# dt's projection in strips of 32 steps beside the gated recurrence, and four of the convolution's sixteen taps on POOL

## The reference

```python
def step(h, xs):                                   # gated recurrence, 128 steps
    z = sigmoid(xzt + h @ U_z + vz)
    r = sigmoid(xrt + h @ U_r + vr)
    hh = tanh(xht + r * h @ U + vh)
    return (1 - z) * h + z * hh
# Mamba block on x = the recurrence's states G
zxbcdt = x @ W_in                                  # 256 z, 384 xBC, 8 dt
dt = softplus(zxbcdt[..., -8:] + dt_bias)
xBC = depthwise_causal_conv(xBC, kernel, taps=16) + conv_b
xBC = silu(xBC)                                    # xs 256, B 64, C 64
dA = exp(dt * A)
h = h * dA + dt * x * B;  y = h @ C + D * xs       # a scan over the steps
y = y * silu(z);  y = rms_norm(y) * norm_w;  t = y @ W_out
x = x + (t / sqrt(1 + t * t)) @ W_nl + b_nl + G
```

## Time and profile before

| | us |
|---|---|
| median of three runs | 2279.24 (2276.68 to 2282.23) |
| profiled execution, its own time | 2276.11 |
| its span from first to last instruction | 2274.4 |
| recurrence | about 30 to 249 |
| Mamba block | about 249 to 700 |
| the rest | about 700 to 2274 |

### The profile page before, as it was taken

The page is one execution under the profiler, slowest core; times in us unless marked ns, Lnnn a source line. Parts: engine busy times, 40 slices in busy tenths (PEclk is TensorE's granted clock), DMA queues, the critical chain, the costliest instruction groups (busy, mean ns, idle before and its releaser), DMA issues.

```text
span 2274.4 us, 74250 instructions
## 1 busy us (share of the span) xinstructions
PE 2000.1 (88%) x31569; PEld 1323.4 (58%) x31675; DVE 1705.3 (75%) x3808; ACT 1001.4 (44%) x2827; POOL 458.8 (20%) x793
## 2 busy tenths in 40 slices
PE   7888888998886888787799999985999789999998
PEld 5555534444454555553567677763666456677776
DVE  3444489999965878787888888843999668888887
ACT  2333236566652121221455555542554445555555
POOL 2211000000000434335012122243432112121200
PEclk9999699999978899898899999996999999999999
DMA  2000000000010000000311111106553211111111
GB/s 61 4 3 4 1 1 1 1 1 1 1 38 17 2 3 2 3 3 2 111 48 44 44 44 44 39 4 128 107 108 73 65 40 44 39 44 44 44 57 37
DMA packets 76083, 77.35 MB, mean 34 GB/s; under 512 B 15756, under 2 KB 57060, under 8 KB 74180
## 3 DMA queue, kind: packets, MB, share of 16 engines
q1 hardware_dynamic: 71848, 70.11, 12.1%
q10 hardware_dynamic: 3904, 2.49, 0.4%
HBM read 60.09 MB, written 11.82 MB: 32 GB/s over the span
## 4 chain that ended last, share of the span: by engine, by line
PE 24%; DVE 18%; ACT 6%; issue 5%; DMA 1%; ACTq 1%; SPq 1%; POOL 1%; another core or an unknown queue 0%; POOLq 0%; DVEq 0%
PE B L85 23%; DVE work L2097 4%; DVE hr L2061 3%; DVE work L2105 3%; DVE work L107 2%; ACT hr L103 2%; ACT ltc L103 2%; ACTq L2384 1%; ACT catt L103 1%; DVE lth L107 1%; DVE lh L107 1%; DVE lpq L107 1%; ACT work L103 1%; DVE gr L1911 1%; DVE work L1471 1%
## 5 line engine op out<-in xcount | busy, mean ns | idle before, releaser
L85 PE MATMUL B<-gr,wres 128*128 128x512 f32 x1248 | 353.3, 411 | 16.4 <-DVE work L2105 10.2
L103 ACT ACTIVATE work<-B 128x512 f32<-128x512 f32 (+5 forms) x460 | 233.3, 524 | 124.4 <-PE B L85 69.3
L2147 POOL COPY G<-lh 128x32 f32<-128x32 f32 x256 | 148.2, 579 | 680.3 <-DVE lh L107 680.3
L85 PE MATMUL B<-work 128*128 128x128 bf16 (+3 forms) x1408 | 259.6, 312 | 28.3 <-ACT work L103 7.0
L85 PEld LDWEIGHTS B<-gr,wres 128*128 128x128 f32 x1248 | 214.2, 189 | 83.4 <-DVE work L2105 27.8
L103 ACT ACTIVATE hr<-work 128x512 fp32r<-128x512 f32 x272 | 172.9, 636 | 146.6 <-DVE work L2105 76.7
L85 PEld LDWEIGHTS B<-work 128*128 128x128 bf16 (+2 forms) x1408 | 141.3, 127 | 138.8 <-issue 79.5
L2061 DVE TENSOR_TENSOR hr<-work,hr 128x512 fp32r<-128x512 f32 x272 | 186.5, 686 | 8.1 <-ACT hr L103 6.6
L2097 DVE TENSOR_TENSOR work<-work 128x512 f32<-128x512 f32 x256 | 178.7, 698 | 14.0 <-ACT work L103 6.6
L107 DVE SCALAR_TENSOR_TENSOR work<-work,cw 128x512 f32<-128x512 f32 x240 | 179.2, 746 | 5.9
L85 PE MATMUL B<-hr,wres 128*128 128x512 f32 x624 | 177.9, 394 | 1.0 <-DVE hr L2061 1.0
(11 more groups left out here) (254 smaller groups left out, 3790.2 us busy)
## 6 DMA issues: line engine op xcount, KB each, us to landing
work<-wdr SPq DMA_DIRECT2D x128, 256.0 KB, 3.1
scr<-catt SPq DMA_DIRECT2D x144, 64.0 KB
work<-scr SPq DMA_DIRECT2D x16, 384.0 KB
work<-scr SPq DMA_DIRECT2D x16, 192.0 KB
catt<-in_L_ffn_ew SPq DMA_DIRECT2D x24, 128.0 KB, 2.4
work<-scr SPq DMA_DIRECT2D x16, 128.0 KB
out<-work SPq DMA_DIRECT2D x32, 64.0 KB, 2.2
work<-in_x ACTq DMA_DIRECT2D x2, 512.0 KB, 5.3
```

Of the source, the lines that this page charges most:

```text
L85: return e.matmul(out, lhsT, rhs, start=start, stop=stop, skip_group_check=True)
L103: return e.activation(out, in_, func, bias=bias, scale=scale)
L2147: e.tensor_copy(self.G[:, :, t], self.lh[:, t % 4, :]).then_inc(*inc("l.pool", "h", li, t))
```

## The change

- The convolution's taps are split 5 + 4 + 7 (`NT, NP = 5, 4`): PE makes five, POOL four, DVE seven. POOL multiplies each shifted tile by its tap with a `tensor_scalar` and adds it, three `tensor_tensor` for a tile, into one of two new buffers `cps`; a wait stands between each two. DVE waits for POOL's sum (`conv.pool`), adds it to `cvb` with one 128x512 `tensor_tensor`, and goes on with taps 9 to 15. The memsets of the pads stay.
- dt's projection is made in strips of 32 steps: from step 32 on each step of the recurrence has one matmul for one sequence and the quarter of the steps that is complete (`mdt_strip_pe`); the last quarter's 32 follow after the last step. The results lie in columns 128 to 192 of banks 1, 3, 5 and 7, so DVE's one addition of the bias becomes four, and the first taps on bank 7 wait for them.
- The warming matmul has 320 columns instead of 384 (it left these banks' columns 128 to 192 free), and in the last eight steps it is doubled where the step isn't a fourth one.
- h0's transposes go to bank 2 instead of bank 1. POOL's additions of G to X stand further back in POOL's order.

```diff
@@ -136,7 +136,7 @@
          "L0_cond_C_z", "L0_cond_C_r", "L0_cond_C")
 EXPERTS = (("L0_ffn_kernel_gating_EDF", "L0_ffn_kernel_up_EDF", "L0_ffn_kernel_down_EFD"),
            ("L1_ffn_ew1", "L1_ffn_ew2", "L1_ffn_ew3"))
-NT = 6
+NT, NP = 5, 4
 COND2_LAG = 22
 MAMBA_DT_TURNS = 6
 MAMBA_UNIT_TURNS = ((8, 1, 1, 1), (22, 1, 1, 1))
@@ -438,14 +438,20 @@
                 e.wait_ge(*at("gru.q", t))
                 mmh(e, NR, o, self.gn[:, 1, :], self.gq[:])
                 mmh(e, NZ, o, self.gn[:, 0, :], self.gq[:])
-            self.gru_warm_pe(e, t, 1)
+            self.gru_warm_pe(e, t, 1 if t < T - 8 or t % 4 == 0 else 2)
+            if t >= 32:
+                if t == 32:
+                    e.wait_ge(*at("ld.mamba"))
+                if t % 32 == 0:
+                    e.wait_ge(*at("gru.g", t - 1))
+                self.mdt_strip_pe(e, t // 32 * 32 - 32, t % 32)
             yield
 
     def gru_warm_pe(self, e, t, n):
 
         B = self.gru_banks(t // 8 * 8 + 9 - t % 8 // 4)[1]
         for _ in range(n):
-            mm(e, B[:, 128:512].rearrange("p (a c) -> p a c", a=3), self.identb[:], bc(self.identb[:], 1, 3), t < 4, True)
+            mm(e, B[:, 192:512].rearrange("p (a c) -> p a c", a=5), self.identb[:], bc(self.identb[:, 0:64], 1, 5), t < 4, True)
 
     def gru_condition_act(self, e, g, odd, bank):
 
@@ -546,6 +552,9 @@
             m |= {"xdt": ar(128, 256), "cbm": ar(128, 128), "y4": ar(128, 4, 256), "sq": self.area(c, [128, 256]),
                   "ss": ar(128, 4), "yT": ar(128, 2, 512), "tm": ar(128, 512)}
             self.mw.append(m)
+        self.cps = [self.area(c, [128, 512]) for _ in range(2)]
+        self.cpt = self.area(w, [128, 512])
+        assert w[1] <= 74 * 256 - 3 * NT * 128
 
     def mprep_load(self, e):
         I = self.I
@@ -572,7 +581,7 @@
             yield
         e.wait_ge(*self.at("ld.mamba"))
         for c in range(2):
-            last = e.transpose(self.bank[1][0:64, c * 128:c * 128 + 128], self.h0[:, c, :], self.ident[:])
+            last = e.transpose(self.bank[2][0:64, c * 128:c * 128 + 128], self.h0[:, c, :], self.ident[:])
         last.then_inc(*self.inc("mprep.h0"))
 
     def mprep_act(self, e):
@@ -583,7 +592,7 @@
         for _ in range(T - 20):
             yield
         e.wait_ge(*self.at("mprep.h0"))
-        act(e, self.h0T[:], self.bank[1][0:64, 0:256], ACT.Copy, scale=0.5).then_inc(*self.inc("mprep.act", "h0"))
+        act(e, self.h0T[:], self.bank[2][0:64, 0:256], ACT.Copy, scale=0.5).then_inc(*self.inc("mprep.act", "h0"))
 
     def mprep_dve(self, e):
         at, inc = self.at, self.inc
@@ -607,20 +616,28 @@
         e.wait_ge(*at("mprep.act", "A"))
         ts(e, self.alog[:], self.alog[:], -1.0, ALU.mult).then_inc(*inc("mprep.dve", "A"))
 
+    def mdt_bank(self, b):
+
+        return self.bank[4 * ((b // 8 + 1) % 2) + 2 * (1 - b % 8 // 4) + 1]
+
+    def mdt_strip_pe(self, e, r, b):
+
+        o = 128 + b // 16 * 32 + b % 4 * 8
+        return mm(e, self.mdt_bank(b)[r:r + 32, o:o + 8], self.G[:, b, r:r + 32], self.win[:, 640:648], False, True)
+
     def mdt_pe(self, e):
         at, B = self.at, self.bank[0]
         e.wait_ge(*at("gru.g", T - 1))
         e.wait_ge(*at("mprep.dve", "A"))
         e.wait_ge(*at("mprep.act", "h0"))
-        P = B[:, 0:256].rearrange("p (b h) -> p b h", h=8)
         for b in range(NB):
-            last = mm(e, P[:, b, :], self.G[:, b, :], self.win[:, 640:648], True, True)
+            last = self.mdt_strip_pe(e, 96, b)
         last.then_inc(*self.inc("mdt.pe", "x"))
         for _ in range(12):
             yield
         e.wait_ge(*at("mdt.dve", "a"))
         e.wait_ge(*at("const", "tri"))
-        P2 = B[:, 256:512].rearrange("p (b h) -> p b h", h=8)
+        P2 = B[:, 0:256].rearrange("p (b h) -> p b h", h=8)
         mm(e, P2, self.tri[:], self.adt, True, True).then_inc(*self.inc("mdt.pe", "c"))
 
     def mdt_act(self, e):
@@ -630,16 +647,19 @@
         for _ in range(12):
             yield
         e.wait_ge(*at("mdt.pe", "c"))
-        P2 = self.bank[0][:, 256:512].rearrange("p (b h) -> p b h", h=8)
+        P2 = self.bank[0][:, 0:256].rearrange("p (b h) -> p b h", h=8)
         act(e, self.ec, P2, ACT.Exp).then_inc(*self.inc("mdt.act", "c"))
 
     def mdt_dve(self, e):
 
         at, then = self.at, self.then
-        P = self.bank[0][:, 0:256].rearrange("p (b h) -> p b h", h=8)
         x, ex, z, q, a = self.dth, self.q1, self.q2, self.q3, self.adt
         e.wait_ge(*at("mdt.pe", "x"))
-        then(e, e.tensor_tensor(x, P, bc(self.dtb[:], 1, NB), ALU.add), "mdt.dve", "x")
+        xs = x.rearrange("p (a c i) h -> p c a i h", a=2, i=4)
+        for c in range(4):
+            P = self.mdt_bank(4 * c)[:, 128:192].rearrange("p (a i h) -> p a i h", a=2, i=4)
+            last = e.tensor_tensor(xs[:, c], P, bc(bc(self.dtb[:], 1, 4), 1, 2), ALU.add)
+        then(e, last, "mdt.dve", "x")
         stt(e, ex, x, -1.0, x, ALU.mult, ALU.min).then_inc(*self.inc("mdt.dve", "e"))
         yield
         e.wait_ge(*at("mdt.act", "e"))
@@ -677,8 +697,7 @@
                 yield
                 yield
                 e.wait_ge(*at("conv.x", n))
-                if n:
-                    e.wait_ge(*at("conv.b", n - 1))
+                e.wait_ge(*(at("conv.b", n - 1) if n else at("mdt.dve", "x")))
                 for k in range(NT):
                     last = mm(e, BT[:], self.tap[:, c * NT + k, :], X[:, :, 1 + k:129 + k], k == 0, k == NT - 1)
                     if k == 2:
@@ -754,9 +773,12 @@
                 if n:
                     silu(n - 1)
                 e.wait_ge(*at("conv.b", n))
-                for k in range(NT, 16):
-                    if k > NT:
-                        e.wait_ge(*at("conv.acc", n, k - 1))
+                e.wait_ge(*at("conv.pool", n))
+                e.tensor_tensor(self.cvb[u % 4][:, c, :], self.cvb[u % 4][:, c, :], self.cps[n % 2], ALU.add).then_inc(
+                    *inc("conv.p", n))
+                yield
+                for k in range(NT + NP, 16):
+                    e.wait_ge(*(at("conv.acc", n, k - 1) if k > NT + NP else at("conv.p", n)))
                     stt(e, acc, X[:, :, 1 + k:129 + k], self.cw[:, c, k:k + 1], acc, ALU.mult, ALU.add).then_inc(
                         *(inc("conv.acc", n, k) if k < 15 else inc("conv.acc", n)))
                     if (15 - k) % 3 == 0 and k < 15:
@@ -767,11 +789,34 @@
         yield
 
     def conv_pool(self, e):
-        e.wait_ge(*self.at("xt", 7))
+
+        at, inc = self.at, self.inc
+        e.wait_ge(*at("xt", 7))
         for x in self.XP:
-            e.memset(x[:, :, 0:16], 0.0).then_inc(*self.inc("conv.pad"))
-        return
-        yield
+            e.memset(x[:, :, 0:16], 0.0).then_inc(*inc("conv.pad"))
+        yield
+        n = 0
+        for u in range(8):
+            for c in range(3):
+                X, P, tmp = self.XP[n % 3], self.cps[n % 2], self.cpt
+                yield
+                e.wait_ge(*at("conv.x", n))
+                if n >= 2:
+                    e.wait_ge(*at("conv.p", n - 2))
+                for k in range(NT, NT + NP):
+                    to = P if k == NT else tmp
+                    ts(e, to.rearrange("p (b t) -> p b t", b=4), X[:, :, 1 + k:129 + k], self.cw[:, c, k:k + 1],
+                       ALU.mult).then_inc(*inc("conv.pt", n, k))
+                    e.wait_ge(*at("conv.pt", n, k))
+                    if k > NT:
+                        e.tensor_tensor(P, P, tmp, ALU.add).then_inc(
+                            *(inc("conv.ps", n, k) if k < NT + NP - 1 else inc("conv.pool", n)))
+                        if k < NT + NP - 1:
+                            e.wait_ge(*at("conv.ps", n, k))
+                for _ in range(3):
+                    yield
+                n += 1
+            yield
 
     def mamba_turns(self, wk, i):
         for _ in range(MAMBA_UNIT_TURNS[wk][i]):
@@ -1044,8 +1089,15 @@
             yield
 
     def mamba_pool(self, e, wk):
+
+        for _ in range(MAMBA_DT_TURNS + 7):
+            yield
         for i in range(4):
             ub = UNITS[wk + 2 * i]
+            for _ in self.mamba_turns(wk, i):
+                yield
+            for _ in range(24):
+                yield
             e.wait_ge(*self.at(f"mw{wk}.dve", "X", i))
             e.tensor_tensor(flat(self.X, ub), flat(self.X, ub), flat(self.G, ub), ALU.add).then_inc(
                 *self.inc(f"mw{wk}.pool", "X", i))
```

## The result

The changed kernel takes 2309.9 us (median, 2309.5 to 2310.7) against 2278.0 of the kernel before: ratio 1.0138, 95% interval 1.0121 to 1.0156, some 32 us slower. The direction was forecast; the forecast size, 107 us, was three times too much. The profiled execution has a span of 2308.9 us, 34.5 more than before's.

What follows compares the result with a forecast made beforehand. DVE was taken to bound the Mamba block. From the profiled execution, 2276.1 - 9.9 (front) - 38.9 (taps) + 156 (POOL blocking DVE) = 2383 us; predicted median 2385 us, range 2315 to 2450.

Steps and rivals of the forecast that it cites:

- The bound: Block's middle, 374 to 611 us: DVE is full, so a microsecond taken from or added to it counts fully.
- Strips behind the recurrence: dt's projection after the recurrence: the last 32 matmuls take 3.5 us instead of 13.82, DVE's four additions about 0.9 us.
- front: Start of the Mamba block, where DVE waits for dt's projection, then runs its chain: -9.9 us in all.
- Strips beside the recurrence: In the recurrence, 96 steps get one strip matmul each and a shorter warming: cost nothing, bounded by 5 us.
- rival D: In the recurrence the shorter warming loses PE's clock: +32 us, 2417 us in all; chance 5%.
- Taps: Convolution: DVE drops three of ten taps and gains one addition; 1.62 us a tile, -38.9 us over 24 tiles.
- The port: Convolution: POOL instructions reading SBUF lock out DVE's two-SBUF operations while they run, 0.96 us an addition, 1.18 a tensor_scalar; +156 us.
- Rival B: Convolution: POOL's tensor_scalar is short, 0.53 us like a memset; 24 tiles cost DVE 83 us, 2313 us in all; chance 13%.
- Rival A: Convolution: POOL runs beside DVE without slowing it, so the 156 us fall away: 2230 us, faster; chance 7%.
- Rival C: Block's stretches: PE, less busy, falls to a lower clock; priced at +50 us, about 2435 us in all; chance 13%.
- The signs: Five expectations for the changed profile, among them DVE taps near 1.3 us and three-tile stretches near 61 us instead of 47.
- Sign 5: In the changed profile, the granted clock stands at 1.00 in the recurrence.

Runs made afterwards that it cites:

- products only: The changed kernel without POOL's three additions of a tile, its four products kept: 2256.3 us, ratio 0.9880 to the kernel before.
- halved additions: The changed kernel with each of POOL's 512-column additions made as two of 256: 2300.6 us, ratio 1.0088 to the kernel before.
- the strips alone: The changed kernel with the convolution as before (six taps on PE, ten on DVE, none on POOL): 2280.75 us, ratio 1.0001 to the kernel before.

## Why the prediction was right or wrong

- **The bound.** Right: DVE was full in the block, and the stage's time followed DVE's work both ways: more of it in the changed kernel, less with memsets, with products only and with halved additions.
- **Strips behind the recurrence.** 3.5 us forecast, 3.58 measured; additions 0.9 forecast, 0.61 measured; front -9.9 forecast, -10.05 in the strips alone. In the changed kernel POOL's first tile takes 7.8 of it back in dt's chain (first tap after 24.8 us instead of 17.0, 0.7 of it DVE's own new addition), which the forecast had in the price of the first five tiles.
- **Strips beside the recurrence.** "Cost nothing" was right for the strips (steps of 1.70 us at the full clock in both) but not for the shorter warming, which I had as rival D at 32 us and a 5% chance: it costs some 4 us, an eighth of that. Between 90 and 235 us the granted clock was 1.00 in the changed kernel and in all four profiled executions with 384 columns; two of the eight with 320 had 0.95 and 0.94. That speaks for rival D's mechanism without showing it.
- **Taps.** -38.9 us fits: between the first and the last tap DVE's inflation is 66 us and its busy time grew by 29, which leaves 37 us of work that disappeared.
- **The port.** The mechanism was right, and so was the price of an addition (0.96 forecast, 0.91 measured) and the length of the tensor_scalar (1.49 forecast, 1.565 alone). The step that failed is "a tensor_scalar 0.96 + (1.49 - 1.27) = 1.18 us": it took for granted that POOL holds the port for as long as it runs. It costs a two-SBUF operation 0.315 us. With that alone put right, a tile costs 4 x 0.315 + 3 x 0.91 = 4.0 us in the first five and, by the same shares, 0.7 x 0.315 + 0.22 x 0.17 = 0.26 for a tensor_scalar (0.17 = 0.65 scaled by 0.315/1.18) and 0.73 for an addition, 3.2 us, in the nineteen others: 20 + 61 = 81 us instead of 156, and 2279 - 48.8 + 81 = 2311 us. Measured: 2310. That they agree to 1 us is partly luck: in the profiles POOL cost DVE 73 us, not 81, and 9 us of the loss lie outside the block.
- **Rival B** had the right number (2313) for the wrong reason: the tensor_scalar is not short, it holds the port shortly. The range's low end, 2315, stood for a tensor_scalar near its shortest length and lay 5 us above the measured time. The prediction held the affine_select of the earlier trace rows up as a second case of full blocking (DVE's operation ended 0.03 us after it); its kind was not among those measured here, and it did not carry over to a tensor_scalar.
- **Rival A** is out: with memsets in POOL's place the kernel is 27 us faster than before, with POOL's reads 32 us slower.
- **Rival C.** The clock in the block's middle fell to 0.93, not to 0.77, and DVE stayed the bound.
- **The signs.** A tap's mean was to be near 1.3 us and came to 1.04; a stretch 61 us and came to 51 (102.5 for two). Both hung on the same term. Sign 5, a clock of 1.00 in the recurrence, held between 90 and 235 us; between 30 and 90 us it was 0.77, against 0.94 and 0.83 in before's two profiles.

## What to carry to other kernels

Where DVE is the bound, ask of each instruction given to POOL not how long it runs there but what it takes from DVE's operations beside it: here a tap moved to POOL as a product and an addition cost DVE 0.315 + 0.91 us and relieved it of 0.78, so by these prices no number of taps pays in this form; other forms of a tap on POOL were not run. Measure this price for the very kind of instruction in a small program of its own, at the tile's size, against each kind that DVE has there. And before a few microseconds of a part are believed or doubted, profile the unchanged kernel twice: here its stages moved by 3 to 7 us between two executions.

## What the runs showed of the hardware that was not expected

- A POOL tensor_scalar of 128x512 runs 1.565 us but costs a DVE operation with two SBUF inputs 0.30 to 0.32 us; a POOL copy that runs 0.61 us costs 0.23; a POOL addition of 1.26 us costs 0.91, one of half the columns (0.72 us) only 0.345; a tensor_scalar of 1024 columns (2.84 us) 0.74.
- The same POOL tensor_scalar costs DVE's in-place fp32 tensor_scalar 0.78 us, and a memset, which costs the two-SBUF operation nothing, costs that one 0.30. The Trainium skill, "SBUF — State Buffer", section "SBUF: two separate sides", says that the pair is locked "for the whole instruction". The trace agrees on who blocks whom, a memset being free for the two-SBUF operation included, but not on the whole instruction: by it a tensor_scalar would have cost more than an addition.
- POOL loses less than DVE: beside two-SBUF operations its tensor_scalar went from 9.86 to 10.98 us for six, its addition from 7.96 to 9.60.
- 32 fp32 matmuls with 32 columns of weights, all in one column strip, take 3.58 us at a granted clock of 0.50 (the lower level, 1.2 GHz), a quarter (26%) of the 13.82 us of those with 128 columns at the same clock, and 2.36 us in the strips' second profile, where it was 0.86; the cost here went by weight columns almost exactly.
